# TensorE's visits in the attention stage of a macaron block behind every second score step

## The reference

```python
def _L0_attn_ref(x, Wqkv, Wo):          # x is the normalised input
    qkv = x @ Wqkv.T
    q, k, v = ...                       # 16 heads of 16
    q = cos * q + rotate_half(q) * sin
    k = cos * k + rotate_half(k) * sin
    scores = jnp.einsum('bhqd,bhkd->bhqk', q, k) / math.sqrt(DH)
    scores = jnp.where(causal, scores, -jnp.inf)
    attn = jax.nn.softmax(scores, axis=-1)
    out = jnp.einsum('bhqk,bhkd->bhqd', attn, v)
    return out.transpose(0, 2, 1, 3).reshape(b, t, d) @ Wo.T
x = x + _L0_attn_ref(_layernorm(x, axis=-1), L0_attn_Wqkv, L0_attn_Wo)
```

## Time and profile before

| | us |
|---|---|
| median of 3 runs | 2367.55 |
| lowest and highest | 2365.91, 2371.05 |
| the profiled execution | 2366.41 |
| its span in the trace | 2364.7 |
| attention stage, one sample (four slots) | 45.36 |

### The profile page before, as it was taken

The page is one execution under the profiler, slowest core; times in us unless marked ns, Lnnn a source line. Parts: engine busy times, 40 slices in busy tenths (PEclk is TensorE's granted clock), DMA queues, the critical chain, the costliest instruction groups (busy, mean ns, idle before and its releaser), DMA issues. The chain is left out here.

```text
span 2364.7 us, 53376 instructions
## 1 busy us (share of the span) xinstructions
PE 2146.5 (91%) x18188; PEld 1163.7 (49%) x18188; DVE 1919.6 (81%) x3961; ACT 1358.4 (57%) x2567; POOL 1276.5 (54%) x1459
## 2 busy tenths in 40 slices
PE   2999999589999999999999999999999986999999
PEld 1666666324444444444444444444444433666666
DVE  4777777469989998998998999899899855777776
ACT  2555555136666676666666666666666663455453
POOL 3666666335545554554554555455455425666664
PEclk9999999679999999999999999999999987999999
DMA  5566666333444454444454445444444413666664
GB/s 157 179 200 200 202 202 202 97 66 89 94 96 91 94 102 94 90 96 89 98 96 92 91 97 101 91 90 97 94 99 95 77 37 128 201 201 200 202 201 163
DMA packets 280350, 295.31 MB, mean 125 GB/s; under 512 B 45744, under 2 KB 263184, under 8 KB 280080
## 3 DMA queue, kind: packets, MB, share of 16 engines
q1 hardware_dynamic: 279536, 290.85, 48.6%
q10 hardware_dynamic: 544, 1.05, 0.1%
HBM read 140.08 MB, written 83.89 MB: 95 GB/s over the span
## 5 line engine op out<-in xcount | busy, mean ns | idle before, releaser
L818 ACT ACTIVATE at_probs<-at_st_ps 128x512 f32<-128x512 f32 x1280 | 748.1, 604 | 468.7 <-PE at_st_ps L923 462.1
L753 DVE TENSOR_REDUCE at_mx<-at_mx_ps 128x1 f32<-128x512 f32 (+3 forms) x1408 | 838.0, 633 | 142.9 <-PE at_mx_ps L905 142.9
L675 POOL TENSOR_SCALAR_AFFINE_SELECT at_probs<-at_probs 128x512 f32<-128x512 f32 x512 | 319.0, 635 | 679.2 <-ACT at_probs L818 675.4
L923 PE MATMUL at_st_ps<-at_q_stack,at_k_stack 49*128 49x512 f16 (+3 forms) x2048 | 461.3, 303 | 73.0 <-ACT at_probs L818 70.9
L900 PE MATMUL at_mx_ps<-at_k_stack,at_q_stack 48*128 48x512 f16 (+3 forms) x2048 | 493.8, 304 | 21.0 <-DMA at_k_stack<-qk_image 11.5
L431 ACT ACTIVATE f_h<-f_h_ps,f_b1s 128x512 f32<-128x512 f32 x256 | 176.0, 688 | 358.6 <-PE f_h_ps L473 347.1
L923 PEld LDWEIGHTS at_st_ps<-at_q_stack,at_k_stack 49*128 49x128 f16 x2048 | 136.6, 94 | 462.1 <-ACT at_probs L818 338.8
L905 PE MATMUL at_mx_ps<-mask,turn 64*128 64x128 bf16 (+2 forms) x1408 | 342.6, 243 | 0.0
L940 PE MATMUL at_pv_ps<-at_probs,at_v 128*32 128x512 f32 (+3 forms) x4096 | 333.7, 444 | 0.0
L489 PE MATMUL f_y_ps<-f_w2hi,f_hhi 128*128 128x256 f16 x1024 | 279.2, 273 | 0.0
L489 PE MATMUL f_y_ps<-f_w2lo,f_hhi 128*128 128x256 f16 x1024 | 279.2, 273 | 0.0
(11 more groups left out here) (117 smaller groups left out, 3903.1 us busy)
## 6 DMA issues: line engine op xcount, KB each, us to landing
at_q_stack<-qk_image SPq DMA_DIRECT2D x192, 128.0 KB, 4.5
at_k_stack<-qk_image SPq DMA_DIRECT2D x192, 128.0 KB, 4.7
f_x<-in_x SPq DMA_DIRECT2D x32, 512.0 KB, 5.6
f_w1hi<-w_hi SPq DMA_DIRECT2D x128, 128.0 KB, 2.5
f_w1lo<-w_lo SPq DMA_DIRECT2D x128, 128.0 KB, 2.2
f_b2s<-in_b SPq DMA_DIRECT2D x128, 128.0 KB, 3.8
f_w2hi<-w_hi SPq DMA_DIRECT2D x128, 128.0 KB, 4.2
f_w2lo<-w_lo SPq DMA_DIRECT2D x128, 128.0 KB, 4.3
```

Source lines behind the costliest of these rows:

```text
L675: nc.gpsimd.affine_select(out=ap, in_=ap, compare_op=ALU.is_ge, fill=0.0, base=0, pattern=[[0, d] for d in dims] + [[1, P]], channel_multi ...
L753: nc.vector.tensor_reduce(o_ap, i_ap, AX_X, ALU.max).then_inc(max_done, 1)
L818: nc.scalar.activation(probs[:, c, :], st_ps[c % 2][:], ACT.Exp, scale=DH ** -0.5).then_inc(exp_done, 1)
L923: ins = nc.tensor.matmul(bank[:, col:col + T - q0], k_stack[ss.par][rows, j + ha, kt * P:(kt + 1) * P], q_stack[ss.par][rows, j + ha, q0:T ...
```

## The change

The steps stay as they are; the visits move on TensorE, and on VectorE and ScalarE the pieces that belong to them. TensorE now makes its visits behind steps 1, 3, 5, 7 and 9 (and 10 for the second part of `project_o`): behind 1 the turned maxima and both halves of the first projection (or two pieces of the values, or the eight transposes), behind 3 the late probs_v, behind 5 half a projection (or a piece of the values, or transpose_o) and turn_output, behind 7 the second half (or a piece of the values), and behind 9 the early probs_v. VectorE does the first rope_low behind reduction 0 as before and the second behind 4 instead of 3, the normalisation behind 6 instead of 5, and the second begin_rope behind 8 instead of 6; the low halves are one reduction later. ScalarE copies the output behind exponential 4 instead of 3, and takes its high halves one exponential later.

```diff
 # VectorE
-                    if g in (1, 2) and sample(s + 1) and n in (0, 3):
-                        rope_low(s + 1, 2 * (g - 1) + (n == 3))
-                    if group(G - 3) and n == 5:
+                    if g in (1, 2) and sample(s + 1) and n in (0, 4):
+                        rope_low(s + 1, 2 * (g - 1) + (n == 4))
+                    if group(G - 3) and n == 6:
                         normalise_output(s, g)
-                    if g < 2 and sample(s + 1) and n in (2, 6):
-                        begin_rope(s + 1, 2 * g + (n == 6))
+                    if g < 2 and sample(s + 1) and n in (2, 8):
+                        begin_rope(s + 1, 2 * g + (n == 8))
...
-                    if g == 3 and sample(s + 2) and n in (1, 2):
-                        low_of(xT.lo, xT.hi, s + 2, n - 1, xT_hi, xT_lo)
-                    if g == 3 and sample(s + -1) and n in (5, 7):
-                        low_of(oT.lo, oT.hi, s + -1, int(n == 7), oT_hi, oT_lo)
+                    if g == 3 and sample(s + 2) and n in (2, 3):
+                        low_of(xT.lo, xT.hi, s + 2, n - 2, xT_hi, xT_lo)
+                    if g == 3 and sample(s + -1) and n in (6, 8):
+                        low_of(oT.lo, oT.hi, s + -1, int(n == 8), oT_hi, oT_lo)
 # ScalarE
-                    if g in (1, 2) and sample(s + 1) and n in (0, 2):
-                        rope_high(s + 1, 2 * (g - 1) + (n == 2))
+                    if g in (1, 2) and sample(s + 1) and n in (0, 3):
+                        rope_high(s + 1, 2 * (g - 1) + (n == 3))
...
-                    if group(G - 3) and n == 3:
+                    if group(G - 3) and n == 4:
                         act.wait_ge(pv_done, 4 * (G - 2))
...
-                    if g == 3 and sample(s + 2) and n in (0, 1):
+                    if g == 3 and sample(s + 2) and n in (1, 2):
...
-                    if g == 2 and sample(s + 1) and n in (4, 7):
-                        v_copy(s + 1, int(n == 7))
-                    if g == 3 and sample(s + -1) and n in (4, 5):
+                    if g == 2 and sample(s + 1) and n in (3, 8):
+                        v_copy(s + 1, int(n == 8))
+                    if g == 3 and sample(s + -1) and n in (5, 6):
...
 # TensorE
-                    if n == 2 and before:
-                        probs_v(s, g, 3, 1, 1)
-                    if n == 1 and group(G - 1):
-                        turn_maxima(s, g)
-                    if n == 2 and before:
+                    if n == 1:
+                        if group(G - 1):
+                            turn_maxima(s, g)
+                        if g < 2 and nxt:
+                            project_qk(s + 1, 2 * g, half=False)
+                            project_qk(s + 1, 2 * g, half=True)
+                        if g == 2 and nxt:
+                            project_v(s + 1, 0)
+                            project_v(s + 1, 1)
+                        if g == 3 and aft:
+                            transposes(s + 2)
+                    if n == 3 and before:
+                        probs_v(s, g, 3, 1, 1)
                         probs_v(s, g, 3, 2, 3)
                         probs_v(s, g, 3, 3, 2)
-                    if n == 5 and before:
-                        turn_output(s, g)
-                    if g < 2 and sample(s + 1) and n in (0, 1, 4, 5):
-                        project_qk(s + 1, 2 * g + (n > 3), half=(n in (1, 5)))
-                    if g == 2 and sample(s + 1) and n in (0, 1, 4, 5):
-                        project_v(s + 1, (0, 1, 4, 5).index(n))
-                    if g == 3 and sample(s + 2) and n == 0:
-                        transposes(s + 2)
-                    if run and n == 8:
+                    if n == 5:
+                        if g < 2 and nxt:
+                            project_qk(s + 1, 2 * g + 1, half=False)
+                        if g == 2 and nxt:
+                            project_v(s + 1, 2)
+                        if g == 3 and old:
+                            transpose_o(s + -1, s)
+                        if before:
+                            turn_output(s, g)
+                    if n == 7:
+                        if g < 2 and nxt:
+                            project_qk(s + 1, 2 * g + 1, half=True)
+                        if g == 2 and nxt:
+                            project_v(s + 1, 3)
+                    if n == 9 and run:
                         probs_v(s, g, 2, 0, 0)
-                    if g == 3 and sample(s + -1) and n == 4:
-                        transpose_o(s + -1, s)
-                    if g == 3 and sample(s + -1) and n >= 9:
+                    if g == 3 and old and n >= 9:
```

More of the change, by code:

```diff
@@ L1021, in slot @@
                 before = group(G - 3)
+                nxt, aft, old = sample(s + 1), sample(s + 2), sample(s + -1)
                 for n in range(11):
```

4 lines of the change are left out of this document (2 added, 2 removed).

## The result

The changed kernel takes 2459.85 us (median of 4 runs, 2456.44 to 2462.95), the kernel before on the same chip 2367.3 (4 runs, 2365.91 to 2371.05): ratio 1.0393, 95% interval 1.0378 to 1.0407, 92.6 us slower. The profiled execution took 2457.75 us, its span is 2456.0.

The account below looks back on a forecast made before the run. TensorE (91% busy) and VectorE (81%) were both candidates, slot 1 full on VectorE. Slots of 10.0, 12.1, 12.4 and 14.1 sum to 48.6 us against 45.36; +3.26 over 30 samples, +98 on 2366.4, gives 2464, range 2375 to 2480.

Parts of the forecast that it names:

- Slots: Attention stage, one sample: slots 0 to 3 walked out at 10.0, 12.1, 12.4, 14.1 us, together 48.6 against 45.36.
- The gain at step 8: Slots 0 to 2: scores behind pairs of steps no longer wait at step 8, removing 0.52 us.
- begin_rope behind reduction 8: Start of slots 1 and 2: reductions 9 and 10 come late behind it, turn_maxima goes at 11.86 instead of 10.66, 1.2 us.
- The blocked rope_low: Slots 1 and 2: rope_low starts 0.2 to 0.3 us into GpSimd's rotated and is blocked, 0.9 us lost in each.
- Rival 1: Rope_low slips in before rotated; slots 1 and 2 lose only waits for reductions: 46.7 us a sample, 2406; chance 0.25.
- rivals 2 and 3: Rival 2: VectorE keeps up, 2335, chance 0.13. Rival 3: that gain meets slot 3's loss, no change, 2365, chance 0.07.
- the prediction's objection: Against the skill's exclusive port lock: it would also block reductions and low halves, none stretched in the trace; no size.
- The copy of the output: Slot 0: turn_output needs ScalarE's copy, now behind exponential 4, so TensorE waits 0.5 us.
- Slot 3: Last slot of a sample: gains and waits sum to +0.95 on 13.11, giving 14.1 us.
- project_o's wait: Slot 3: project_o needs the second oT low half, now behind reduction 8, 10.64 against 10.12 for TensorE, +0.6.
- Transpose_o: Slot 3: it waits for the second xT low half, whose high half is one exponential later, +0.45.
- The clock: TensorE's granted clock stays at the higher level despite new waits of about 1.2 us; called no rival, no chance given.

Follow-up runs that it names:

- the mixed order: Kernel before with projection's last piece (slots 0-2) behind step 7, second begin_rope behind 8, first rope_low behind reduction 2: 2366.1 us; slot 1's second rope_low also behind 2: 2353.9.

## Why the prediction was right

The forecast was 2464 us, the measured median is 2459.85. Step by step:

- **Slots.** 10.0, 12.1, 12.4 and 14.1 us were walked out, 9.98, 12.02, 12.33 and 14.01 came: 48.34 against 48.6. Each slot is within 0.1 us of its walk, so the sum is not right by errors that cancel between slots.
- **The gain at step 8.** It went as said: slots 0 to 2 no longer wait at step 8. TensorE's own idle time on exponentials fell from 2.1 to 1.0 us a sample, so of the 256.5 us that the prediction quotes only about a fifth was there to be had; most of that wait ran beside matmuls. What is left is in slot 3, in front of steps 8 and 9, where single steps follow each other:

```profile
1099.11 0.28 PE L923 MATMUL at_st_ps<-at_q_stack,at_k_stack 49*128 49x256 f16 x1 [0.52 <-ACT at_probs L818]
...
1100.08 0.28 PE L923 MATMUL at_st_ps<-at_q_stack,at_k_stack 49*128 49x256 f16 x1 [0.47 <-ACT at_probs L818]
```

- **begin_rope behind reduction 8.** The order of events was right (M1 waits for r9, the turn for r10), and so was the time: from M0 to the turn in slot 1 the row shows 1.73 us, the walk had 1.86. What the walk took for a cost of its own, this wait, is not one: with the turn moved away (2475.85) M3 waited longer instead and was no earlier, and with the old order of TensorE the late begin_rope cost nothing (2366.36). It is VectorE's backlog, and can be paid in either place.
- **The blocked rope_low.** This was the step that no row of before carried: rope_low 0.2 to 0.3 us into rotated. It came 0.19 into it and took 1.63 us; the walk had 1.6. Two runs price it at 43 and 50 us; the walk's 0.9 us in two slots for 30 samples is 54. The difference is mostly in slot 2, which got back only 0.63 of its 0.95 us. Rival 1, rope_low in first, is excluded by that row, and rivals 2 and 3 by the waits for r9, r10 and r1. The Trainium skill, "SBUF — State Buffer", section "SBUF: two separate sides", says that only a VectorE instruction with two SBUF inputs (or in a two-port mode) meets GpSimd there and that the order of issue decides who blocks; the rows agree, rope_low, with two SBUF inputs, being stretched and the low halves and reductions, which read PSUM, not; the prediction's objection, that by the rule reductions would be blocked too, holds only against the short form of it in section Terms.
- **The copy of the output.** Named once, 0.5 us in slot 0. It is in slot 1 too: turn_output waits 45 times between 700 and 1800 us, two a sample, and begins 0.4 us later than TensorE was free for it. The walk had it there without a name (turn_output at 18.0 with TensorE free at 17.6). The run with the copy back in its place gave back 33 us, 26 of them in slots 0 and 1 of 30 samples and 5 in the last samples, which the prediction left out. As a cost of the change this term is larger than the prediction's text lets one think, and it is the one that was cheapest to avoid.
- **Slot 3.** +0.95 was said, of which +0.6 for project_o's wait. The stretch is 0.90 longer, and undoing all of slot 3 gave 25 to 27 us, some 0.9 a sample; the low half alone gave 13 us, 0.44 a sample. The rows of TensorE show project_o at 1053.67, 0.48 behind the 1.00 of the early probs_v at 1052.19, so this term was 0.12 too large. Transpose_o waited 0.4 us for its low half, where +0.45 was said.
- **The clock.** It stayed at 1.00 in all four slots, as said. The new idle times were shorter than said, 0.70 us at most in front of one matmul instead of 1.2. That the clock was no rival held for this kernel alone: with begin_rope behind reduction 10 TensorE stood idle for 1.48 us at M3, and in part of the slots the granted clock fell.

With the block gone, slots 1 and 2 take 11.07 and 10.92 us by the turns, against 11.05 and 10.98 in the kernel before. What is left of the loss then lies in the intervals of slots 0 and 3, 0.57 and 0.85 us longer; that of slot 0 holds the copy's wait and the waits for r9 and r10 in front of the turn of slot 1. No run takes these last waits away and leaves all else in place.

## To carry to other kernels

When a visit of the matrix engine moves, walk the in-order queues of the engines that serve it, from the piece that moved to the next two waits of the matrix engine: what stands behind it there is where the time goes, even if nothing new is computed. An elementwise operation on VectorE with both inputs in SBUF should be started where GpSimd has nothing running; here such placements cost the changed kernel 43 to 50 us, and mending one of them took the mixed order from 2366.1 to 2353.9. Moving a wait to another instruction of the same queue gains nothing as long as the engine that it waits for is late for all of them.

## What the runs showed of the hardware

- **The end of a blocked operation goes with the other's end.** A rope_low that began in the first microsecond of by_sin or rotated ended 0.54 to 0.56 us behind their end, in all runs: it took 1.63 when it began 0.19 into rotated, and 1.32 when it began 0.49 into by_sin. It isn't only these two: in the kernel before, a rope_low that began under a mask of GpSimd took 0.81 and ended 0.54 behind it. But one that began 0.2 us into GpSimd's smallest operation (128x4, L699, 1.02 us long) took its usual 0.68. An operation with a PSUM input isn't touched: the reductions at 1067.43, 1.87 us for three, ran over by_sin at their usual 0.6 each.
- **It isn't one-sided.** GpSimd's next operation is slower while a stretched rope_low still runs: in the kernel before, rotated took 1.52 us over the end of the rope_low of 499.75, where 1.27 is usual.
- **The clock fell without a long pause.** With begin_rope behind reduction 10, an idle time of 1.48 us went ahead of the fall to the lower level, in some slots and not in others with the same wait. The changed kernel, where TensorE's own longest wait between 700 and 1800 us is 0.7 us, shows 1.00 in all four slots.
